# A fused eight-batch attention and FFN kernel: mask row added by VectorE, context loaded transposed, GpSimd's long operations whole, a new order of steps

## The chip, the cores and the metric

The kernel runs on one core of one Trainium2 chip. Its engines are TensorE (PE, with its weight loads as PEld), VectorE (DVE), ScalarE (ACT), GpSimd (POOL) and SyncE (SP), which here only issues DMAs. ACT issues some DMAs too. The metric is the time of one execution on the device in microseconds (us).

## The reference

The reference takes x and a context (both 8 batches x 256 rows x 256 columns, fp32) and a mask row per batch (8 x 256), and applies eight layers to each batch on its own:

```
L0: x += attention(norm(x), ctx), 16 heads    x += top-2-of-8 experts(norm(x)), experts 256x256
L1: x += attention(norm(x), ctx) under a fixed 256x256 mask     x += 3 coupling steps, each a small net
L2: x += linear attention(norm(x), ctx)       x += lin(norm(x)) + gated low-rank experts
L3: x += softmax(q k^T / sqrt(d) + (mask - 1) * 10000) v        x += down(silu(gate) * up), 768 hidden
```

Every attention takes its keys and values from the context. The mask row is the same for all 256 query rows of its batch.

## The kernel before

A batch is 256 rows, held as 2 tiles of 128 partitions (T = 2) with 256 columns; a transposed matrix is 2 column blocks (KT = 2) of 128 partitions with 256 columns. A projection of a batch is four fp32 matmuls on PE, which the trace shows as two records each.

**Threads and order.** On each engine the work is cut into steps by Python generators ("threads"), and `weave` takes one step of a thread after another as a written list says (`TURNS`, lines 89 to 134, one string per engine, one letter per step). The threads: p = `prep` (norm of x, keys, queries and values of the first attention of each batch, the linear attention's context part `third`, keys and values of the second attention), s = `score` (maxima of the head scores, the experts, queries of the second attention), v = `value` (scores again, exponentials, values, output of each attention), a = `net` (the coupling steps and the linear attention), b = `rest` (L2's FFN and all of L3) for batches 0 to 6, c = the same for batch 7 in two halves, w and z = filler matmuls of zeros on PE (line 1986), which keep it running. An engine runs its list strictly in order, so a step whose wait isn't met holds all behind it.

**First attention's context (what the change touches).** `next_cin` (SP, line 499) loads the context of batch b into `cin`. PE's `prepare` (line 1546) starts with `transpose_all` (line 1505) of it, four 128x128 transposes into PSUM; ACT's `prepare` (line 797) copies the result to `ctxT[b % 4]` with a 128x512 copy (`evac`, line 738; the copy is line 740). Buffer b % 4 is free when `rest` of batch b - 4 has done its last read (semaphore `r3_ps`, line 1881). From `ctxT` come all keys and values; `cin` itself is read only by `third` (line 1524).

**Keys and queries** are split into three bf16 parts. ACT makes the first part and an fp32 copy from PSUM; GpSimd makes the others (`split_k`, line 614, `split_q`, line 627): three operations, each once for every column block of 256 columns, so six instructions. SP then writes the parts to a scratch in HBM (line 460) and reads them back as rows of `KA` (line 475) and `QA` (line 493), and the heads of `score` (line 1611) wait for that. For batch 0 the rows are copied directly (`first_keys` by ACT's queue, lines 791 to 795; `first_queries` by SP, line 512, in which SP first waits for the keys to land).

**Norms.** GpSimd's `norm` (line 602) waits for the statistics, makes the reciprocal deviation by two small operations and then, in the same step, waits until DVE has used it (`xh_s`), before it can go on.

**The mask.** In `rest`, DVE turns the mask row, loaded to all 128 partitions, into an additive row and adds a term of the bias (lines 1409 and 1413). PE adds it to the scores by a third matmul, whose weights are the matrix `first` with ones in its first row:

```
for kk in range(KT):
    pe.matmul(ps, L.xhBT[:, kk, t * P:(t + 1) * P], L.k3[:, kk, :], start=(kk == 0), stop=False)
last = pe.matmul(ps, W("first"), L.mrow[:, :], start=False, stop=True)
```

DVE then takes the row maxima by one reduction (line 1446). The attention under the fixed mask has the form that the change takes over: `tensor_tensor_reduce` (line 1169) adds a mask tile to the PSUM scores in place and gives the maximum.

**Large loads.** The packed weights come in seven loads (0 to 3 by SP, 4, 5 and 6 by ACT, line 736); `wi`, the integer weights of L3's FFN, by ACT at line 840, and `dequantize` (line 955) turns it to fp32 in 18 steps.

Of the kernel before, what the change touches and what calls it, by code (L numbers as in the profile page):

```python
# [14 lines left out]
P = 128  # L15
# [28 lines left out]
def cantor_mask():  # L44
# [27 lines left out]
    ("gw3", P, 1), ("aq", P, KT * P), ("first", P, P), ("bao", P, D), ("lin", P, KT * D), ("blin", P, D),  # L72
# [5 lines left out]
for _e in PACK:  # L78
    if _e == "cut":
        CUTS.append(_at)  # L80
    else:
# [17 lines left out]
        "vvbvpsbsabppbaavabavbvvavbvvvbvvvabvpvvbvvabavavvpvvapvavabapvavpvvvvavavvvpsvvvvbvbvvvbvpvvvbvsbbsp"
        "aapvapbavbvavvbavvbvvvvbvvabpavavbvvapvvvvpavavabapavvpavvavvsvvbpvvvbvvbvvpvvvvvvvbvsbbsapapbvapbav"  # L100
        "bvavvbvvavvbvvaabvpvbvvvavvavvavpvvapbavavapvvvpvvavvvavvsvpbvvbvvvbpvvvvbvbsbsapappavbavbavvvvvabvv"
        "vvbvvvvvbvapvbavvbvppvaavpavavapsabavvvvvvaavvvvpbvvvvvbvvvbvvspvsbavbvbvapvvppvbvavbvvavabpvpvvvvav"
        "bvvvvbavavabbvavvavvsvaaabavvvvvaavvvvvbvvsbvvsvvbvcbabbaavavbavvbvavbvvabvavbavbavvvvvavbvavaaavvbv"
        "aavbaabaaaaaabaaaaaaaaabaaaaaaaaaaaaabbaaaabbcccbcbcbcbccbcccccccccccccccccc",
    "vector":
        "ppppppvppppvppppssssssssssssssssssvssvvpvpvpvspspsssssssssssppsssssssssspsssssbssssssssvsvsssssssbpv"
        "svpsssspvsssssssspssvssvsvpvssvasasssssspsssssasasasssssspsspssssvsssssssssasvasapvsppvssssvssaaaaas"
        "apsaabssbvsbpvbbsbbssbbvsvssbbvbaabsssssbbssbssaaassbpssbsssbsssbspsbssssvbsaasvsabssssvvspssvssaaaa"
        "abssapssspapbabsbssbvbbsbbbsbsbbvsbsvpvsssbvpaasbsssbsssbssssbasaabssssbppssbsssbspbsvssasasssbasvss"
        "vsvssssvaaaaabassssbaspabbspspbbbbbbbvsbbssbvsssvsvsbspvapabbssbsssssssbssbaasasbsssbssssspbspbvssss"  # L110
        "vaasabsssvsvsspvssssabaaaasassspsababbpsbsbvbbspbbvbsbsbssbsvsvssbpvapabbsssbsssssssssbsaaassssbsssp"
        "ssbpsssvsbsssbssssvbsvpsvsaaassvbssssaaasaabapsssaabbbpsvbsbsbbbbbpssssvbvbvbvsaspassssbspsssbsbsbss"
        "ssspbsssaaabsvssbsvsssbssssvsvsssbvssbssassaasbssaasaaasbsassababbsssvvsbbbbbbbvvpbbbvaabcssssbsbsbs"
        "sssaaabssbssscbsbsssbaasavbbaaaaavavvbababvabaaabbbbbbbaaaabbbaaaabaaaaaaaaaabbaabacacccbcccccbccccc"
        "bccccbcbcccccbccccccccbcccccccccccccc",
    "tensor":
        "pwwwpppwwwppwwwwwwwppwwwwwwwwwwwwwwwwwwwwwwwwwwwwwwpwwwwwpwpwwwwwwwwppwwwwwwwwwwwwsswpsspssvpsvswwvs"
        "wvvsswwsvswwvpsvvpvpvssvvvvpvpvvvvwwwvwwwvwwwvvwwwwvpvwwvpvvpwwwwwwwpwspsssssssssssssssssppbspsspbps"
        "sbsspssbvssvbssvvpvsbvsbvsspvvbsvpsvpvvvvsspvsvvssvvpvssvsvsvswvpvssvwsvvsswwvwsvpvvpvsvsvsvvsvssvss"
        "vvvvsvspvvsvvsvsvsvvsvsvsvsvvpwwppwaasasspasspsassavsvspsssvvpvpvssavssvvavavssvvspsvsvpvspvvsasvvss"  # L120
        "spavspsavssvvasvpaavspvsavvavavpsvvsvssvsavpsvavvsavsvvvvsvbsvvbvvssvssvssvvsvbsvbpvbvsvpsbsbbaspsas"
        "sbabbvssapavssbapsbbvvssavbbvasvbsvbvpvssavbsbvvsbvbvvapsvsbvsbapsavbsbvbbsvbsvbsvavsavavbsvsbavavap"
        "svsbvppsbvsvpvpvabvavvpvsavssvvvvsbvssbvsssspvvssbvssvbvbssvvpbvsvsbvbvpsvsbsbpasbsasaspspsvassbavps"
        "bbvvasvbsbvpsabbvassvvavsbvbsvvvbsvvbspsababapvspvsbvvbsvbsbsbvbsvsvabsasvavbspvsavavabvpvbpssbvavpa"
        "vpvasvpssvsbvvsbvspvvvbvsvbvbsvvsvssvssvsssvvsbsvbvbvpvsvsbpsbbapssaasppsbsasvbssvbapsbbvasvvsbbvspa"
        "vsbvvbvssavabsbssavvbpvbvpavbvpvvsbsbsvabvsbvbsasvvavsbvavssbvvsavspasvbabvvpvpbsvspvapvvavpvsavvvsb"
        "svbsvsvssvvsvpvsbsbbsvssvsvsbsvssvpbvbsvvbpssbbaspasapsspsasvbsavssbsabvvspvpsvsbavbsvvsavsbvbsvsvvs"
        "vbsvbvvsavspsbvsabspvpsbbvssavvbvbvssabbsvpbvvsabavavpabpsvvabpabspvssvbsvsavvsvasbpvasvvsvbsvbvsvvs"
        "vvssvssvsbvvbbsvpvsvsvvbsspbssbaspsvavsabvpsbbvssvppsavsbsvpsvbpvbavsspvpbbavvvavpvsbvsvsbvvsavsbvsa"
        "vbssvsavsbvsasvbsvvbsbvsasvbbbbbbvavsvbaavssvsabasassbssvbssvvssvbasassvavvvssvvpbvvbvsvsvsvvbvbvbvc"  # L130
        "cvvbcbbacassbassbbavssavscbsavbvbvsasvbbvsavasbbsvavbbasvsbsabvvvvbvabvvavvabvbbabvbabazbbvvbvabvavb"
        "avvzzzzzzzzzbzzzabaaaaazzzzzaaabaaabbaaaaaaaaabaabaabaaaaaaaaaaazzzzzzzzzzzbzzzbbaaaazzzaazzbzzzbbcc"
        "ccbbzzzzzzbbczzzzzzbbzccbbcbbzczzzzcccbcbcccbbbcbccccccccccccccccccccccccccccccc",
# [43 lines left out]
def program(nc, x_in, ctx_in, mask_in, pack, nomask, ipack, scratch, out):  # L177
    ctx = ExitStack()
    with ctx:
# [171 lines left out]
        ctx_ps, ctx_t = sem("ctx_ps", 1), sem("ctx_t", 1)  # L351
# [99 lines left out]
        def _(sp):  # L451
# [118 lines left out]
            def rest():  # L570
                sp.dma_start(mrow[:, :], mask_in[0:1, :].to_broadcast([P, S])).then_inc(m_in_s, 16)
                yield
                for b in range(B - 1):
                    if b + 1 < B - 1:
                        sp.wait_ge(sc_ps, nth(sc_ps, b, 1))
# [7 lines left out]
            sp.dma_start(cin[:, :, :], rows(ctx_in, 0)).then_inc(c_in_s, 16)  # L583
            load(0)
            load(1)
            load(2)
# [7 lines left out]
        def _(pool):  # L594
# [7 lines left out]
            def norm(t, b, n):  # L602
                pool.wait_ge(stats[t], nth(stats[t], b, n))
                link(t, pool.tensor_tensor(veps[t][:, :], mv[t][:, :, 1], epsm[:, :], ALU.add))  # L604
                pool.tensor_tensor(rstd[t][:, :], veps[t][:, :], powm[:, :], ALU.pow).then_inc(rstd_s[t], 1)
                pool.wait_ge(xh_s[t], nth(xh_s[t], b, n))

            def norm_part(t, b, n, h, lo, hi):
# [3 lines left out]
                pool.wait_ge(xh_s[t], of(xh_s[t], b, n, h))  # L612

            def split_k(b, m):
                pool.wait_ge(k_f[m], nth(k_f[m], b, 1))
                for k in range(KT):
                    pool.tensor_tensor(kparts[:, k, 1, :], kf[:, k, :], kparts[:, k, 0, :], ALU.subtract)  # L617
                for k in range(KT):
                    last = pool.tensor_tensor(kf[:, k, :], kf[:, k, :], kparts[:, k, 0, :], ALU.subtract)
                link("p", last)  # L620
                yield
                for k in range(KT):
                    last = pool.tensor_tensor(kparts[:, k, 2, :], kf[:, k, :], kparts[:, k, 1, :], ALU.subtract)
                last.then_inc(k_split[m], 1)
                yield

            def split_q(b, m, t):
                f, parts = qf[m], qparts[m]
                pool.wait_ge(q_f[m], nth(q_f[m], b, 1))
                for k in range(KT):  # L630
                    pool.tensor_tensor(parts[:, k, 1, :], f[:, k, :], parts[:, k, 0, :], ALU.subtract)
                for k in range(KT):
                    last = pool.tensor_tensor(f[:, k, :], f[:, k, :], parts[:, k, 0, :], ALU.subtract)
                link(t, last)
                yield
                for k in range(KT):
                    last = pool.tensor_tensor(parts[:, k, 2, :], f[:, k, :], parts[:, k, 1, :], ALU.subtract)
                last.then_inc(q_split[m], 1)
# [7 lines left out]
            def prepare(b):  # L646
                norm("p", b, 1)
                yield
# [17 lines left out]
            def score():  # L666
                for b in range(B):
                    norm("s", b, 1)
                    yield
                    pool.wait_ge(xh_s["s"], nth(xh_s["s"], b, 1))  # L670
                    for i in range(T):
                        last = pool.tensor_tensor(x[:, i, :], x[:, i, :], xh[:, i, :], ALU.add)
                    last.then_inc(xe_s, 1)
                    yield
                    norm("s", b, 2)
                    yield
# [57 lines left out]
        def _(act):  # L734
# [1362 lines left out]
```

## Time and profile before

| | us |
|---|---|
| three runs | 995.49, 996.83, 1000.37 (median 996.83) |
| the profiled execution | 996.77 |
| its span, first to last instruction | 995.0 |
| PE busy | 957.1 (96%) |
| DVE, ACT, POOL busy | 631.2, 537.3, 235.2 |
| mean granted TensorE clock | 0.997 of full |

All rows below are of this one execution. Times are microseconds from the start of the span unless marked ns. "PE busy" counts fillers as well. A row of the order of time gives start, length, engine, line, operation, output and inputs, shape and how many instructions were merged; square brackets hold the idle time before it and who ended it.

### The profile page before, as it was taken

How to read it: one execution, taken by the hardware profiler on the slowest of the kernel's cores; microseconds unless marked ns; L12 is line 12 of the kernel's file. 1: busy time of each engine (PE TensorE's matmuls, PEld its weight loads, DVE VectorE, ACT ScalarE, POOL GpSimd, SP SyncE). 2: the span in 40 equal slices, each digit the busy share in tenths (PEclk: the TensorE clock that was granted, in tenths of full speed). 3: DMA queues.
4: the chain of work that ended last, by engine and by line, in shares of the span. 5: the costliest groups of instructions: out<-in, count | busy, mean ns of one | idle time of the engine just before them, and what ended most of it. 6: DMA issues, size and time to landing. Idle time of an engine off the chain costs nothing.

```text
span 995.0 us, 17737 instructions
## 1 busy us (share of the span) xinstructions
PE 957.1 (96%) x6202; PEld 711.6 (72%) x6202; DVE 631.2 (63%) x2222; ACT 537.3 (54%) x1103; POOL 235.2 (24%) x418
## 2 busy tenths in 40 slices
PE   8899889989999999999999999999999999999998
PEld 7665565656587867777587766777687867878777
DVE  4634673577677775767576776875676566736554
ACT  1341646496458643766357743776378444864421
POOL 3104402311340241413231043313131113001200
PEclk9999989999999999999999999999999999999999
DMA  7308823120523121402134023402122004000000
GB/s 249 45 14 235 217 49 70 42 55 2 106 49 64 44 53 33 101 11 49 27 68 77 12 48 71 101 17 67 25 43 59 28 1 91 1 13 1 1 1 22
DMA packets 39927, 56.25 MB, mean 57 GB/s; under 512 B 3968, under 2 KB 35712, under 8 KB 36224
## 3 DMA queue, kind: packets, MB, share of 16 engines
q1 hardware_dynamic: 38448, 46.50, 22.8%
q10 hardware_dynamic: 1392, 8.63, 2.4%
q8 instruction: 50, 0.82, 0.4%
q14 instruction: 37, 0.30, 0.1%
HBM read 39.64 MB, written 13.89 MB: 54 GB/s over the span
## 4 chain that ended last, share of the span: by engine, by line
PE 73%; ACT 9%; DVE 6%; DMA 4%; issue 4%; POOL 2%; SPq 1%; ACTq 0%; DVEq 0%; POOLq 0%
PE bank L1639 10%; PE bank L1966 7%; PE bank L1696 6%; PE bank L1499 6%; PE bank L1718 5%; PE bank L1490 5%; PE bank L1977 4%; PE bank L1611 4%; PE bank L1753 4%; PE bank L1747 3%; PE bank L1699 2%; ACT PT L871 2%; PE bank L1508 2%; ACT QA L858 2%; PE bank L1779 2%
## 5 line engine op out<-in xcount | busy, mean ns | idle before, releaser
L871 ACT ACTIVATE PT<-bank 128x512 f32<-128x512 f32 x256 | 153.2, 598 | 140.2 <-PE bank L1699 78.3
L1639 PE MATMUL bank<-w,xhT 128*128 128x512 f32 x256 | 125.2, 598 | 0.0
L1696 PE MATMUL bank<-QA,KA 104*128 104x256 bf16 x512 | 112.8, 273 | 9.2 <-ACT PT L871 6.7
L1169 DVE CUSTOM_DVE_ANT_0 bank<-bank,maskb 128x256 f32<-128x256 f32 x256 | 101.9, 450 | 23.0 <-PE bank L1611 22.2
L1162 DVE TENSOR_REDUCE mx<-bank 128x2 f32<-128x512 f32 x128 | 84.1, 682 | 32.9 <-PE bank L1611 32.2
L1611 PE MATMUL bank<-KA,QA 96*128 96x256 bf16 x512 | 92.9, 275 | 7.6 <-issue 3.0
L1696 PEld LDWEIGHTS bank<-QA,KA 104*128 104x128 bf16 x512 | 46.7, 99 | 57.0 <-issue 45.7
L1966 PE MATMUL bank<-xhBT,wi 128*128 128x256 f32 x336 | 85.2, 384 | 0.7 <-DVE hT L1473 0.3
L1215 DVE SCALAR_TENSOR_TENSOR x<-bank,one,x 128x256 f32<-128x256 f32 x128 | 61.6, 481 | 34.6 <-PE bank L1639 30.0
L858 ACT COPY QA<-bank 8x256 bf16<-8x256 bf16 (+1 forms) x128 | 67.9, 576 | 16.3 <-PE bank L1677 15.0
L1611 PEld LDWEIGHTS bank<-KA,QA 96*128 96x128 bf16 x512 | 47.3, 100 | 31.3 <-issue 6.7
L1966 PEld LDWEIGHTS bank<-xhBT,wi 128*128 128x128 f32 x336 | 58.8, 189 | 10.1 <-DVE hT L1473 3.0
L1699 PE MATMUL bank<-maskb,identb 128*128 128x256 bf16 x256 | 63.5, 273 | 0.0
L1718 PE MATMUL bank<-PT,vaug 128*32 128x256 f32 x1024 | 62.1, 382 | 0.6 <-ACT PT L871 0.6
L1639 PEld LDWEIGHTS bank<-w,xhT 128*128 128x128 f32 x256 | 42.6, 190 | 24.5 <-issue 19.6
L1753 PE MATMUL bank<-xhAT,w 128*128 128x256 f32 (+1 forms) x216 | 49.6, 361 | 1.3 <-ACT xhAT L903 1.0
L1986 PE MATMUL bank<-blank 128*128 128x256 bf16 x348 | 47.0, 282 | 1.1 <-POOL blank L722 1.1
L1718 PEld LDWEIGHTS bank<-PT,vaug 128*32 128x32 f32 x1024 | 29.8, 109 | 24.9 <-issue 7.4
L610 POOL TENSOR_TENSOR veps_a<-mv_a,epsm 128x2 f32<-128x2 f32 (+1 forms) x18 | 3.5, 195 | 171.8 <-DVE mv_a L1052 169.7
L604 POOL TENSOR_TENSOR veps_s<-mv_s,epsm 128x2 f32<-128x2 f32 x16 | 3.2, 197 | 169.6 <-DVE mv_s L1052 168.8
L1264 DVE RECIPROCAL rc<-bank 128x8 f32<-128x8 f32 x64 | 13.0, 204 | 47.5 <-PE bank L1731 47.0
L617 POOL TENSOR_TENSOR kparts<-kf,kparts 128x256 bf16<-128x256 f32 x32 | 20.9, 674 | 90.1 <-ACT kf L756 72.1
(316 smaller groups left out, 2079.8 us busy)
## 6 DMA issues: line engine op xcount, KB each, us to landing
QA<-scratch SPq DMA_DIRECT2D x90, 128.0 KB, 4.4
scratch<-kparts SPq DMA_DIRECT2D x30, 192.0 KB, 2.3
KA<-scratch SPq DMA_DIRECT2D x15, 384.0 KB, 4.6
scratch<-qparts SPq DMA_DIRECT2D x30, 192.0 KB, 2.3
KA<-scratch SPq DMA_DIRECT2D x15, 256.0 KB, 5.5
w<-pack ACTq DMA_DIRECT2D x1, 2409.0 KB, 8.6
wi<-ipack ACTq DMA_DIRECT2D x1, 2304.0 KB, 9.8
xin<-x_in SPq DMA_DIRECT2D x8, 256.0 KB, 5.5
```

Of the source, the lines that this page charges most:

```text
L858: act.copy(QA[m][KR:KM, g * GH + lo:g * GH + hi, :], ot_b16[KR:KM, 512:512 + S].unsqueeze(1).to_broadcast([MR, hi - lo, S])).then_inc(negm ...
L871: act.activation(PT[:, n % RING, :, :].rearrange("p t s -> p (t s)"), st_bank[:, :], ACT.Exp).then_inc(exp_s, 1)
L1162: dve.tensor_reduce(mx[:, i % 4, n % GH, :], s_bank[n % 2][:, :].rearrange("p (t s) -> p t s", t=T), AX.X, ALU.max).then_inc(max_s, 1)
L1169: last = dve.tensor_tensor_reduce(s, s, maskb[:, t, :], op0=ALU.add, op1=ALU.max, scale=1.0, scalar=-HUGE, accum_out=mx[:, i % 4, n % GH, ...
L1215: ins = dve.scalar_tensor_tensor(x[:, t, :], bank[n % 2][:, e * D:(e + 1) * D], one[:, t, k:k + 1], x[:, t, :], ALU.mult, ALU.add)
L1611: last = pe.matmul(s_bank[n % 2][:, t * S:(t + 1) * S], QA[m][0:KR, u, t * P:(t + 1) * P], KA[m][0:KR, u, :], start=True, stop=True)
L1639: last = pe.matmul(bank[n % 2][:, :], xhT[:, kk, t * P:(t + 1) * P], W("exp0", KT)[:, kk, i * 512:(i + 1) * 512], start=(kk == 0), stop=(k ...
L1696: last = pe.matmul(st_bank[:, t * S:(t + 1) * S], KA[m][0:KM, v, t * P:(t + 1) * P], QA[m][0:KM, v, :], start=True, stop=(m == 0))
L1699: last = pe.matmul(st_bank[:, t * S:(t + 1) * S], identb[:, :], maskb[:, t, :], start=False, stop=True)
L1718: last = pe.matmul(pv_bank[32 * h:32 * h + 32, g % 2 * S:(g % 2 + 1) * S], vflat[m][:, t, (g * GH + h) * VW:(g * GH + h) * VW + 32], PT[:, ...
L1753: last = pe.matmul(ps[:, k * S + lo * P:k * S + hi * P], W(name, KT)[:, kk, k * P:(k + 1) * P], src[:, kk, lo * P:hi * P], start=(kk == 0) ...
L1966: last = pe.matmul(ps[:, i * S + lo * P:i * S + hi * P], ww[:, kk, k * P:(k + 1) * P], L.xhBT[:, kk, lo * P:hi * P], start=(kk == 0), stop ...
```

## The change

1. The context also arrives transposed, as an input of its own (`ctxT_in`). SP loads it straight into `ctxT` (eight loads of 256 KB more), and PE's transposes and ACT's copies go. The waits for a free buffer move from ACT to SP. `third` now waits for `cin` itself. At the start `cin` is loaded behind weight load 1, and the transposed context stands in its old place.
2. The mask matmul and the weights `first` go; DVE adds the row with `tensor_tensor_reduce`, one instruction for each half of a batch.
3. GpSimd's split operations and the addition x + xh take both blocks in one instruction of 512 columns.
4. GpSimd's wait for the use of a norm is a step of its own.
5. All five order lists are new.

```diff
 def next_cin(b):
     if b < B:
-        sp.wait_ge(ctx_ps, nth(ctx_ps, b - 1, 1))
+        if b >= CTX:
+            sp.wait_ge(r3_ps, nth(r3_ps, b - CTX, 1))
+        elif b == CTX - 1:
+            sp.wait_ge(qk_ps, 2)
+        if b >= 2:
+            sp.wait_ge(ctx_t[b % 2], nth(ctx_t[b % 2], b // 2 - 1, 16))
+        turned_ctx(b)
         sp.wait_ge(third_pe, nth(third_pe, b - 1, 2))
         sp.dma_start(cin[:, :, :], rows(ctx_in, b)).then_inc(c_in_s, 16)
...
+def turned_ctx(b):
+    sp.dma_start(ctxT[b % CTX][:, :, :].rearrange("p k s -> p (k s)"), ctxT_in[b]).then_inc(ctx_t[b % 2], 16)
...
-    for k in range(KT):
-        pool.tensor_tensor(kparts[:, k, 1, :], kf[:, k, :], kparts[:, k, 0, :], ALU.subtract)
+    pool.tensor_tensor(kparts[:, :, 1, :], kf[:, :, :], kparts[:, :, 0, :], ALU.subtract)
...
-    evac(ctxT[b % CTX], pb if b else lb, ctx_ps, nth(ctx_ps, b, 1), ctx_t)
-    yield
...
-    transpose_all(kb, cin).then_inc(ctx_ps, 1)
-    yield
-    pe.wait_ge(ctx_t, nth(ctx_t, b, 1))
+    pe.wait_ge(ctx_t[b % 2], nth(ctx_t[b % 2], b // 2, 16))
...
-    link(L.t, dve.tensor_reduce(
-        L.m2[:, lo:hi], L.bank[h][:, :].rearrange("p (t s) -> p t s", t=T)[:, lo:hi, :], AX.X, ALU.max))
+    for t in range(lo, hi):
+        ps = L.bank[h][:, t * S:(t + 1) * S]
+        last = dve.tensor_tensor_reduce(ps, ps, L.mrow[:, :], op0=ALU.add, op1=ALU.max, scale=1.0,
+                                        scalar=-HUGE, accum_out=L.m2[:, t:t + 1])
+    link(L.t, last)
...
-    last = pe.matmul(ps, W("first"), L.mrow[:, :], start=False, stop=True)
```

What the new lists say, read letter by letter. PE: 1666 steps for 1680; the order of those that remain is close to the old one (a step shifts by 5 places in the mean, by 103 at most; the first projection of keys of batches 4 to 7 comes some 50 places earlier). Filler steps (two matmuls each): 62 instead of 69 ahead of the first head, 31 in both from there to the experts of batch 0, none in either from there to the first head of attention (0,1), 13 instead of 8 from there on, and 54 instead of 58 at the end. Ahead of the first two heads of attention (1,0) stood the transposes of context 2; now nothing does. ACT: the load of `wi` stood ahead of the exponentials of attention (1,0); now it stands behind the fourteenth of its sixteen, and the first dequantizing step behind the end of that attention. GpSimd: the third key operation of batch 1 stood behind the addition x + xh of the experts of batch 0 and now stands ahead of it; the split of the second attention's keys of batch 0 now starts ahead of the wait for the use of the norm before it. In the new PE list the last read of `ctxT` by `rest` of batch b - 4 stands 82, 64 and 98 places ahead of the first projection of keys of batch b = 5, 6 and 7.

## Rows read from the trace of the kernel before

**Rows 1.** The page: busy time, share of the span, instructions of each engine.

```profile
PE 957.1 (96%) x6202; PEld 711.6 (72%) x6202; DVE 631.2 (63%) x2222; ACT 537.3 (54%) x1103; POOL 235.2 (24%) x418
```

**Rows 2.** Stretches: length, busy time and instructions by engine, clock, DMA share, GB/s.

```profile
75.40:126.30 50.90, 44.07 (x241) 29.11 (x241) 26.05 (x65) 21.13 (x47) 22.23 (x36) 0.99 0.88 222
126.30:250.00 123.70, 114.28 (x757) 76.33 (x758) 79.55 (x307) 75.08 (x151) 26.76 (x46) 0.98 0.21 44
250.00:888.00 638.00, 632.14 (x4067) 473.00 (x4066) 429.51 (x1525) 379.55 (x746) 156.45 (x269) 1.00 0.24 48
```

**Rows 3.** The chain of waits, in order of time: start, length (us), what.

```profile
14.72 3.93 DMA KA<-kparts
```

**Rows 4.** PE in order of time, around the first long stalls.

```profile
103.21 0.66 PE L1508 MATMUL bank<-w,cin 128*128 128x128 f32 x4 [2.22 <-DMA cin<-ctx_in]
103.70 0.60 PE L1611 MATMUL bank<-KA,QA 96*128 96x256 bf16 x4
...
126.31 1.01 PE L1611 MATMUL bank<-KA,QA 96*128 96x256 bf16 x4 [3.03 <-issue]
```

**Rows 5.** The chain of waits between 95 and 116 us.

```profile
95.89 1.31 POOL kparts L617 x2
...
100.27 4.58 DMA scratch<-kparts
...
105.70 10.10 DMA scratch<-qparts
```

**Rows 6.** ACT's queue in order of time: the load of wi.

```profile
105.22 0.41 ACTq L840 DMA_DIRECT2D wi<-ipack  x1
```

**Rows 7.** A stretch of 25 us; after the engines come clock, DMA share, GB/s.

```profile
125.00:150.00 25.00, 22.61 (x155) 15.51 (x156) 19.33 (x94) 10.55 (x25) 0.89 (x2) 0.86 0.23 46
```

**Rows 8.** PE in order of time, last batch: mask matmul and what follows it.

```profile
963.99 0.59 PE L1928 MATMUL bank<-xin,w 128*128 128x256 f32 x2
964.42 1.03 PE L1927 MATMUL bank<-kf,xh0T 128*128 128x256 f32 x4
```

**Rows 9.** DVE groups by line and shape: busy us and mean ns, idle before.

```profile
L1169 DVE CUSTOM_DVE_ANT_0 bank<-bank,maskb 128x256 f32<-128x256 f32 x256 | 101.9, 450 | 23.0 <-PE bank L1611 22.2
...
L1446 DVE TENSOR_REDUCE m<-bank 128x2 f32<-128x512 f32 x7 | 4.8, 684 | 2.2 <-PE bank L1928 2.2
```

**Rows 10.** PE's instructions of line 1881 alone, by stretches of 10 us.

```profile
350.00:360.00 10.00, 1.03 (x4) 0.68 (x4) 1.00 0.04 8
```

**Rows 11.** All engines in order of time, the first 36 us.

```profile
6.51 1.11 PE L1508 MATMUL bank<-w,cin 128*128 128x128 f32 x4 [1.81 <-DMA w<-pack]
...
7.74 0.39 ACTq L736 DMA_DIRECT2D w<-pack  x1
...
8.70 2.20 PE L1490 MATMUL bank<-ctxT,w 128*128 128x256 f32 x8
```

**Rows 12.** DMA issues of the whole span: count, KB each, median us to landing.

```profile
QA<-scratch SPq DMA_DIRECT2D x90, 128.0 KB, 4.4
...
w<-pack ACTq DMA_DIRECT2D x1, 2048.0 KB, 10.2
```

**Rows 13.** SP's queue in order of time: the reads of attention (1,0).

```profile
94.68 2.63 SPq L493 DMA_DIRECT2D QA<-scratch  x6
```

**Rows 14.** GpSimd in order of time around the third key operation of batch 1.

```profile
75.58 1.41 POOL L672 TENSOR_TENSOR x<-x,xh 128x256 f32<-128x256 f32 x2 [0.91 <-DVE xh L1065]
76.94 1.30 POOL L623 TENSOR_TENSOR kparts<-kf,kparts 128x256 bf16<-128x256 f32 x2
```

**Rows 15.** GpSimd groups by line and shape.

```profile
L617 POOL TENSOR_TENSOR kparts<-kf,kparts 128x256 bf16<-128x256 f32 x32 | 20.9, 674 | 90.1 <-ACT kf L756 72.1 <-DVE xh L1065 17.9
...
L604 POOL TENSOR_TENSOR veps_p<-mv_p,epsm 128x2 f32<-128x2 f32 x8 | 1.6, 196 | 87.3 <-DVE mv_p L1052 87.1
```

**Rows 16.** The filler matmuls (line 1986) alone, by stretches.

```profile
126.30:250.00 123.70, 2.73 (x16) 1.51 (x16) 0.98 0.21 44
```

More of the change, by code:

```diff
@@ L99 @@
[L99 to L103, printed above, removed]
@@ L174, in weave, with program @@
             pass
-def program(nc, x_in, ctx_in, mask_in, pack, nomask, ipack, scratch, out):
+def program(nc, x_in, ctx_in, ctxT_in, mask_in, pack, nomask, ipack, scratch, out):
     ctx = ExitStack()
@@ L349, in program @@
         xh_s = {t: sem(f"xh_{t}", n) for t, n in norms.items()}
-        ctx_ps, ctx_t = sem("ctx_ps", 1), sem("ctx_t", 1)
+        ctx_t = [sem(f"ctx_t{i}", 16) for i in range(2)]
         xh0T_ps, xh0T_s = sem("xh0T_ps", 1), sem("xh0T_s", 1)
@@ L582, in _ @@
             sp.dma_start(xin[0][:, :, :], rows(x_in, 0)).then_inc(x_in_s[0], 16)
-            sp.dma_start(cin[:, :, :], rows(ctx_in, 0)).then_inc(c_in_s, 16)
+            turned_ctx(0)
             load(0)
             load(1)
+            sp.dma_start(cin[:, :, :], rows(ctx_in, 0)).then_inc(c_in_s, 16)
             load(2)
@@ L611, in norm_part @@
                 pool.tensor_tensor(rstd[t][:, lo:hi], veps[t][:, lo:hi], powm[:, lo:hi], ALU.pow).then_inc(rstd_s[t], 1)
-                pool.wait_ge(xh_s[t], of(xh_s[t], b, n, h))
             def split_k(b, m):
                 pool.wait_ge(k_f[m], nth(k_f[m], b, 1))
-                for k in range(KT):
-                    pool.tensor_tensor(kparts[:, k, 1, :], kf[:, k, :], kparts[:, k, 0, :], ALU.subtract)
-                for k in range(KT):
-                    last = pool.tensor_tensor(kf[:, k, :], kf[:, k, :], kparts[:, k, 0, :], ALU.subtract)
-                link("p", last)
+                pool.tensor_tensor(kparts[:, :, 1, :], kf[:, :, :], kparts[:, :, 0, :], ALU.subtract)
+                link("p", pool.tensor_tensor(kf[:, :, :], kf[:, :, :], kparts[:, :, 0, :], ALU.subtract))
                 yield
-                for k in range(KT):
-                    last = pool.tensor_tensor(kparts[:, k, 2, :], kf[:, k, :], kparts[:, k, 1, :], ALU.subtract)
-                last.then_inc(k_split[m], 1)
+                pool.tensor_tensor(kparts[:, :, 2, :], kf[:, :, :], kparts[:, :, 1, :], ALU.subtract).then_inc(k_split[m], 1)
                 yield
@@ L629, in split_q @@
                 pool.wait_ge(q_f[m], nth(q_f[m], b, 1))
[L630 to L634, printed above, removed]
+                pool.tensor_tensor(parts[:, :, 1, :], f[:, :, :], parts[:, :, 0, :], ALU.subtract)
+                link(t, pool.tensor_tensor(f[:, :, :], f[:, :, :], parts[:, :, 0, :], ALU.subtract))
                 yield
-                for k in range(KT):
-                    last = pool.tensor_tensor(parts[:, k, 2, :], f[:, k, :], parts[:, k, 1, :], ALU.subtract)
-                last.then_inc(q_split[m], 1)
+                pool.tensor_tensor(parts[:, :, 2, :], f[:, :, :], parts[:, :, 1, :], ALU.subtract).then_inc(q_split[m], 1)
                 yield
@@ L647, in prepare @@
                 norm("p", b, 1)
+                yield
+                used("p", b, 1)
                 yield
@@ L669, in score @@
                     yield
+                    used("s", b, 1)
+                    yield
                     pool.wait_ge(xh_s["s"], nth(xh_s["s"], b, 1))
-                    for i in range(T):
-                        last = pool.tensor_tensor(x[:, i, :], x[:, i, :], xh[:, i, :], ALU.add)
-                    last.then_inc(xe_s, 1)
+                    pool.tensor_tensor(x[:, :, :], x[:, :, :], xh[:, :, :], ALU.add).then_inc(xe_s, 1)
                     yield
                     norm("s", b, 2)
+                    yield
+                    used("s", b, 2)
                     yield
@@ L708, in rest @@
                         norm_lane(L, b, 1, h, lo, hi)
+                        yield
+                        used_lane(L, b, 1, h)
                         yield
@@ L1926, in rest @@
                             for kk in range(KT):
-                                pe.matmul(ps, L.xhBT[:, kk, t * P:(t + 1) * P], L.k3[:, kk, :], start=(kk == 0), stop=False)
-                            last = pe.matmul(ps, W("first"), L.mrow[:, :], start=False, stop=True)
+                                last = pe.matmul(ps, L.xhBT[:, kk, t * P:(t + 1) * P], L.k3[:, kk, :],
+                                                 start=(kk == 0), stop=(kk == KT - 1))
                             if t + 1 < hi:
@@ L2063, in packed @@
         "right": padded(a["L2_ffn_right"].reshape(E * R, D), P, D),
-        "first": padded(np.ones((1, P), np.float32), P, P),
         "wq3t": tiles(a["L3_xattn_Wq"].T), "bq3": column(a["L3_xattn_bq"]),
@@ L2083 @@
         "ctx_in": np.ascontiguousarray(a["ctx_1024"]),
+        "ctxT_in": np.stack([tiles(c.T) for c in a["ctx_1024"]]),
         "mask_in": np.ascontiguousarray(a["mask_BxS2_ff1"]),
```

102 lines of the change are left out of this document (59 added, 43 removed).

## The prediction

> **What bounds the kernel now.** I read first the busy shares and the stretches, then the chain of waits and PE's order of time in the start, then the queues' issues around the one long stall. PE is busy 96% of the span [rows 1]. By stretches [rows 2] it idles 6.83 us in 75.4 to 126.3, 9.42 us in 126.3 to 250 and 5.86 us in the 638 us to 888. Before the first and behind the last of these, filler matmuls (line 1986) count as busy, so there the bound is the chain of waits; from 126.3 to 888 it is PE itself, and every other engine has room (DVE 429.5 of 638 us).
>
> The start has three waits that matter. The first attention's heads wait for rows of KA and QA sent by DMA; the head of that chain is the ACT-issued copy of the first keys, which landed at 18.65 (14.72 + 3.93) [rows 3]. At 103.21 PE, after 2.22 us idle, transposes context 2, and only behind that, at 103.70, does it start the heads of attention (1,0) [rows 4]. And at 126.31, after 3.03 us idle, it starts the heads of (0,1) [rows 4]: their queries' write to scratch took 10.10 us from 105.70 [rows 5], in a stretch where ACT had issued the 2304 KB load of wi at 105.22 [rows 6]. Around that idle the granted clock fell from 2.4 to 1.2 GHz: it was 0.86 in 125 to 150 [rows 7], so 7.0 us were spent at the lower level.
>
> **The change part by part.** The sum is made on the profiled execution: 996.77 us, of which 995.0 is span and 1.77 lies around it; the median of the runs is 996.83.
>
> *Mask matmuls.* 16 leave PE (two a batch). Start to start one costs 964.42 - 963.99 = 0.43 us [rows 8]; the busy column says 0.59 because it overlaps the next. Six batches have theirs between 126.3 and 888: 12 x 0.43 = 5.2 us, on the path as PE is the bound there. The other four (batches 6 and 7) lie after 888 in dense PE work: 1.7 us. Bounds: 0.43 and 0.59 each, so 6.9 to 9.4. In their place DVE reads each half with the add-and-max instruction, 450 ns, and a short read of the accumulator: twice 450 for one reduction of 684 [rows 9], +0.2 to +0.5 us a batch. DVE has 208 us free in 250 to 888 [rows 2], and the lane that waits (rest) has a batch's time of slack, so I count 0; in the last batch, where nothing covers it, 0.2 us, beside 0.86 us of mask there, within the 1.7.
>
> *Context transposes and their copies.* Four transposes a batch: 0.49 us (103.21 to 103.70) [rows 4]. Five batches (3 to 7) have theirs after 126.3: 2.4 us (0.49 and 0.66 each, 2.4 to 3.3). The ACT copy that goes with each leaves an engine with room: 0. In exchange SP issues eight more loads of 256 KB, one a batch. Batches 4 to 7 now wait on SP for the rest lane of four batches before. For batch 5 that lane's last reader of the context ran in 350 to 360 [rows 10]. Counting turns in the new lists, SP is held at this wait for some 30 of them, but what stands next on it (the second queries of batch 3) is not ready before PE has made 66 more turns, and the first keys of batch 5 come 82 turns after the release (a turn is 995/1680 = 0.59 us, so 48 us). For batches 6 and 7 it is 64 and 98 turns. So nothing waits: 0.
>
> *Start, to 37.3.* The projection of the first keys began at 8.70, after transposes at 6.51 and their copy [rows 11]: 2.2 us earlier now. But ACT also issues load 4 (2048 KB) 1.2 us earlier, and it is the same queue that carries the first keys: issued at 7.74 [rows 11], landing 10.2 us after [rows 12], so near 18.1, and the keys landed 18.65. There are also 256 KB more ahead of it. I take 0.3 of the 2.2, bounds -0.6 and 2.2.
> The trace has the keys land 0.5 us behind the load [rows 3, 12]. The Trainium skill, DMA: Bandwidth & Descriptors (Queues, rings and completion order), says that each DMA engine takes the descriptors of one queue in order. By that rule the earlier copy can't pass the load and this term is near 0, the sum 0.3 smaller; were it not so, it is 2.2.
>
> *Heads (1,0).* PE's new order has no transposes there, and the heads no longer stand behind cin: -2.7 us if their QA rows have landed. SP issued these from 94.68 to 97.3 [rows 13]; GpSimd does the third key operation of batch 1 ahead of the 1.41 us addition to x instead of behind it [rows 14], and SP's chain starts from that at 78.3, so all moves 1.4 us up. Such a row takes 4.4 us to land [rows 12], so 101.7 becomes 100.3, and PE is free at 100.99. I take 2.5; bounds 0.4 and 2.7. The price here is 256 KB more in a busy stretch, behind the QA rows.
>
> *Heads (0,1).* In ACT's new list the load of wi stands behind the fourteenth exponential of attention (1,0), past the write that it slowed; PE's heads (0,1) begin before that. Without it the queries' write, 10.10 us, should come near the 4.58 us that the keys' write took just before [rows 5]: 5.5 us, more than the 3.03 us stall plus the 2.5 us that PE comes earlier is worth. I take 2.5 of the 3.03 (0 to 3.0). With the idle goes the low clock: of the 7.0 us at most 1.3 lie in the idle, so some 5.8 us of work ran at half rate, 2.9 us lost; I take 2.5 (0 to 2.9). What is late next: the dequantizing on ACT, which waits for wi and has the next attention's exponentials behind it; some seven heads at 1.2 us lie between, 8 to 9 us against 9.8 us of landing, so up to 1.5 us of stall, inside the bounds.
>
> *GpSimd, whole operations.* An operation on 256 columns takes 674 ns and one on 2 columns 196 [rows 15], so 1.88 ns a column, and 512 take 1.16 us against 1.31 for a pair in the chain [rows 5]. Six pairs are in the chain to heads (0,1), -0.9 us, already inside the terms above; in the PE-bound part 0. Bounds 0 and 1.
> The Trainium skill, GPSIMD Engine Reference (3.1 Elementwise), gives about 2.6 cycles an element at 1.2 GHz for two-input operations; by that slope 512 columns are an estimated 1.30 us and the whole form gains nothing (that chain is 0.9 us later). The trace's slope is lower.
> Waits for xh as turns of their own: they free GpSimd for other work early; the one that stood ahead of the split of the second keys of batch 0 held it till 95.89 [rows 5], under 1 us, which is counted above.
>
> *New order.* Aside from what was said, PE's list is nearly the old one (mean shift of a step 5 turns). Filler turns: 62 for 69 before the first head, 13 for 8 after heads (0,1), 54 for 58 at the end. Five more in the middle cost at most 5 x 0.34 = 1.7 us [rows 16]; as they fill idle time in part I count +0.7.
>
> **Sum:** 0.3 + 2.5 + 2.5 + 2.5 + 5.2 + 2.4 + 1.7 - 0.7 = 16.4 us. 995.0 - 16.4 + 1.8 = 980.4 us; against the median of the runs the same.
>
> **Rivals.**
> A, the stall before heads (0,1) stays, because other traffic (the added context load, cin, xin, the scratch writes) fills the DMAs there anyway: they were busy 88% of 75.4 to 126.3 [rows 2]. PE then only waits longer and the clock falls as before. Lost: 5.0 and, as a start later absorbed, the 2.5 of heads (1,0): 16.4 - 7.5 = 8.9, 988 us. For it: the keys' own write was slow before wi was issued. Against: 10.10 is twice 4.58, and wi is the one large load there.
> B, all bounds at the good end: the mask at 0.59 and the transposes at 0.66, the start's 2.2 whole and the stall whole: 9.4 + 3.3 + 2.2 + 2.7 + 5.9 = 23.5 less 0.7 is 22.8, 974 us. Against: start-to-start times.
> C, the gain is eaten by order. PE's 15.3 us idle between 126.3 and 888 [rows 2] is small because the old list fits the old durations; with steps shifted by up to 100 turns it doubles: 996.8 - 16.4 + 15.3 = 995.7, no change.
> D, slower: SP held at the new wait for the rest lane before the context load of batches 4 to 7. If that lane's r3 step comes so late that the load lands behind the turn of the batch's first key projection, PE stops in order, as at 126.31. Price per stop: 3.03 idle and 2.9 of low clock, 5.9 us, and four of them 23.6: 996.8 - 16.4 + 23.6 = 1004. It decides once r3 comes within some 6 us (issue and landing) of that projection; the count above gives 38 us or more, so little speaks for it.
>
> **How the numbers follow.** The forecast 0.60, A 0.15, B 0.10, C 0.09, D 0.06. The forecast's own range is 976 to 986; with A and half of B, and leaving out C and D, 973 to 991. About 0.5% (5 us) is what a measurement tells from no change: faster holds the forecast, A and B, 0.85; same is C, 0.09; slower is D, 0.06.
>
> **What would show it.** No transposes of cin and no mask matmul on PE; GpSimd operations of 512 columns near 1.16 us; first heads within 1 us of 37.3; heads (1,0) near 101 and heads (0,1) near 120.5 to 121.5 with no fall of the clock; between that and the start of the last batch's tail 7 to 8 us less. Wrong if heads (0,1) still come behind 3 us of idle and a clock of 0.5, if PE idle after them is over 20 us, or if the first heads come 2 us early.

## The result, and the profile after

Four runs of the changed kernel: 984.87 to 987.86 us, median 987.23, beside 998.06 for the kernel before on the same chip: ratio 0.9892 with a 95% interval of 0.9868 to 0.9917, some 10.8 us less. The prediction was 980.4 us (16.4 less), range 973 to 991. The profiled execution took 987.86 us with a span of 986.1.

The busy line of the page after, and the three stretches that answer to [rows 1, 2] (columns as there):

```profile
PE 949.3 (96%) x6126; PEld 702.7 (71%) x6126; DVE 634.1 (64%) x2245; ACT 536.3 (54%) x1097; POOL 221.5 (22%) x317
```

```profile
75.40:126.30 50.90, 48.21 (x257) 32.01 (x257) 30.61 (x86) 21.75 (x48) 17.59 (x20) 0.97 0.68 159
126.30:250.00 123.70, 115.25 (x785) 77.00 (x788) 76.98 (x291) 75.79 (x152) 27.48 (x35) 0.99 0.32 72
250.00:880.00 630.00, 620.83 (x3982) 462.89 (x3973) 431.52 (x1538) 378.78 (x740) 143.59 (x196) 1.00 0.24 49
```

PE's idle time in 75.4 to 126.3 fell from 6.8 to 2.7 us. In the long middle it rose: 9.2 us in 630, where [rows 2] have 5.9 in 638. PE in order of time, at the two places of [rows 4]:

```profile
101.55 0.61 PE L1629 MATMUL bank<-KA,QA 96*128 96x256 bf16 x4
...
120.92 0.60 PE L1629 MATMUL bank<-KA,QA 96*128 96x256 bf16 x4
```

Heads (1,0) start 2.15 us earlier and heads (0,1) 5.4 us earlier, with no idle before them. By about 132 us, where the third attention of batch 2 begins (before: 138.96, now: 131.79), 7.2 us are won. That is four fifths of the 8.9 us by which this span is shorter, in the first seventh of it. At the first matmul of `net`'s last product (line 1829 before, 1847 now) the gain is 8.8 us for batch 6 (898.08 before, 889.33 now) and 7.7 for batch 7.

### The profile page after: what moved, and what is told of

Same layout as the page of the kernel before. It is cut to its first block, busy times and chain, and to the rows that moved or that the text cites. A ratio compares the mean times of both kernels' runs of the same rounds, so it can differ in the third digit from the quotient of the medians.

```text
span 986.1 us, 17493 instructions
## 1 busy us (share of the span) xinstructions
PE 949.3 (96%) x6126; PEld 702.7 (71%) x6126; DVE 634.1 (64%) x2245; ACT 536.3 (54%) x1097; POOL 221.5 (22%) x317
## 4 chain that ended last, share of the span: by engine, by line
PE 77%; ACT 9%; DVE 8%; issue 4%; POOL 1%; DMA 1%; ACTq 0%; SPq 0%; DVEq 0%; POOLq 0%
PE bank L1657 11%; PE bank L1984 6%; PE bank L1517 6%; PE bank L1736 6%; PE bank L1714 6%; PE bank L1508 6%; PE bank L1629 4%; PE bank L1995 4%; PE bank L1771 4%; PE bank L1765 3%; PE bank L1717 3%; ACT PT L886 2%; ACT QA L873 2%; PE bank L1797 2%; PE bank L1526 2%
## 5 line engine op out<-in xcount | busy, mean ns | idle before, releaser
L2004 PE MATMUL bank<-blank 128*128 128x256 bf16 x336 | 44.7, 279 | 1.1 <-POOL blank L743 1.1
L1995 PE MATMUL bank<-wi,hT 128*128 128x256 f32 x168 | 42.2, 382 | 0.1
```

The costliest lines, as they stand in the source:

```text
L1995: last = pe.matmul(ps[:, t * D:(t + 1) * D], hid[:, kk, t * P:(t + 1) * P], wd[:, kk, :], start=(kk == 0), stop=(kk == HT - 1))
```

## The experiments

"Before" and "after" below are the two kernels; ratios are to before, on the same chip. Batches are numbered from 0. A gain "at batch n" is the time by which that batch's first matmul of line 1829 (1847 after) comes earlier than in the profile of before. "Lost clock" is the sum of (1 - granted clock) over windows of 1 us within the span: a fall to 1.2 GHz for 3.4 us loses 1.7.

**Each edit by itself, every list in its old order.** Mask row only (SP's wait before it overwrites the mask row goes with it, from PE's scores to DVE's maxima):

```diff
-    last = pe.matmul(ps, W("first"), L.mrow[:, :], start=False, stop=True)
+    (DVE)  dve.tensor_tensor_reduce(ps, ps, L.mrow[:, :], op0=ALU.add, op1=ALU.max, ...)
```

> The kernel before with one edit: the mask row is added by VectorE in one tensor_tensor_reduce per query tile, and the mask matmul is gone; the order of every engine is the old one. Theory 1 (the terms of the prediction: every mask matmul stood on a path that TensorE sets): 12 x 0.43 us in batches 0 to 6 and 1.7 us in the tail, 6.9 us less, a ratio near 0.993. Rival (TensorE waits for ScalarE's exponentials and VectorE's maxima anyway, so most of the freed time turns idle): under 3 us less, 0.997 to 1.000, with more idle time ahead of the second scores in the waits.

Measured: 0.9981 (0.9964 to 0.9997), 1.9 us less. Transposed context only:

```diff
-    transpose_all(kb, cin)        # and ACT's copy of it
+    sp.dma_start(ctxT[b % CTX]..., ctxT_in[b])
```

> The kernel before with one edit: the transposed context is loaded, TensorE's transposes and ScalarE's eviction of them are gone, the rest of each engine's order is the old one, and the big MLP weight load stays ahead of attention (1,0). Theory 1: 0.3 at the start, 2.4 us for five batches' transposes, up to 2.5 at the heads of (1,0): about 5 us less at the end, 0.995, and the stall before the heads of (0,1) still there, about 3 us long with the clock falling after it. Rival (the start gives its 2 us and the stall takes them, the transposes filled idle time): 0 to 2 us less, 0.998 to 1.000.

Measured: 0.9997 (0.9976 to 1.0018). GpSimd's operations whole only:

```diff
-    for k in range(KT): pool.tensor_tensor(kparts[:, k, 1, :], kf[:, k, :], kparts[:, k, 0, :], ...)
+    pool.tensor_tensor(kparts[:, :, 1, :], kf[:, :, :], kparts[:, :, 0, :], ...)
```

> The kernel before with one edit: GpSimd's splits and its sum whole with 512 columns; each wait for the normalized rows stays in its old place. Theory 1: 0.15 us less per pair (1.16 against 1.31), nothing of it on the path: 1.000, within 0.1%. Rival (the splits of the keys stand on the chain to the heads, and the shared port makes VectorE slower beside a long operation): a change of over 2 us either way.

Measured: 0.9999 (0.9981 to 1.0016). And the three together, still in the old order:

> The kernel before with all three edits (mask row, transposed context, whole operations) in the old order of every engine, the load of the MLP weights in its old place too. Theory 1 (the parts add up): the sum of the three kernels above, by the prediction's terms 12 us less, 0.988, so that the new order with the later load brings little over it, against the 5 us that the stall and its clock were put at. Rival (the parts share one limit, ScalarE's exponentials or the stall): less than the sum, 4 to 7 us less, 0.993 to 0.996, and the new order brings the rest.

Measured: 0.9982 (0.9961 to 1.0004), 1.8 us less. So for the mask and for the context the rival holds, for GpSimd the first theory, and the three together bring less than even their rival's 4 to 7 us: of the 12 us that the terms give the parts, the old lists pay out two. Why is seen where the kernel with the mask edit and the kernel before, whose PE steps stand in the same order, are laid side by side. PE in order of time, near 390 us, before:

```profile
387.41 1.02 PE L1927 MATMUL bank<-hT,xhBT 128*128 128x256 f32 x4
388.27 0.59 PE L1928 MATMUL bank<-mrow,w 128*128 128x256 f32 x2
...
390.44 1.03 PE L1499 MATMUL bank<-w,attT 128*128 128x256 f32 x4
391.31 0.29 PE L1537 MATMUL bank<-w,xh0T 128*128 128x16 f32 x2
391.72 0.66 PE L1508 MATMUL bank<-w,xh 128*128 128x128 f32 x4
```

and the same steps with the mask row on DVE (PE's lines are 3 higher), PE's rows with one each of GpSimd and DVE between them:

```profile
387.19 1.02 PE L1930 MATMUL bank<-hT,xhBT 128*128 128x256 f32 x4
...
389.38 1.13 PE L1502 MATMUL bank<-w,attT 128*128 128x256 f32 x4
389.99 0.69 POOL L605 TENSOR_TENSOR rstd_s<-veps_s,powm 128x2 f32<-128x2 f32 x1
390.35 0.29 PE L1540 MATMUL bank<-w,xh0T 128*128 128x16 f32 x2
390.71 0.73 DVE L1065 TENSOR_SCALAR xh<-x,mv_s,rstd_s 128x256 f32<-128x256 f32 x2 [1.15 <-POOL rstd_s L605]
391.50 0.66 PE L1511 MATMUL bank<-w,xh 128*128 128x128 f32 x4 [0.86 <-DVE xh L1065]
```

The lead is 0.22 us ahead of the mask step and 1.06 behind it: the 0.84 us are really won. Three steps later PE stands 0.86 us for DVE's normalized rows `xh`, and the lead is 0.22 again. Those rows are the end of a chain (the last expert's matmuls, DVE's sum and statistics, GpSimd's rstd, DVE's scaling) that started from PE ahead of the mask step and is as much earlier as PE was there; the mask matmuls lay under that chain. In the kernel before, the rows were ready at 391.67 and PE came for them at 391.72: the list fitted to 0.05 us. The same is seen in the other batches: each gains 0.4 to 0.9 us at its mask step and meets a wait soon after, for `xh` at 613 us (0.73), for `xhA` at 729 and 840 us (0.47 and 0.63); only near 500 us some 0.3 us are kept. In that kernel PE waits 1.6 us for `xh` and 1.1 for `xhA` between 250 and 880 us, for which before it did not wait, and the milestone's gain goes from 0.2 at batch 1 to 0.4 at batch 5, with eight mask matmuls (3.4 us) gone between. The rival named other waits, for ScalarE's exponentials and VectorE's maxima; those hardly changed (2.3 us for the exponentials before, 2.4 now).

**The load of wi.** The kernel before, the load some ten steps later in ACT's list:

```diff
-  "...bbsspbsvvbvvvpvpvpvvvvpvvvvvb..."
+  "...bbsspbvvbvvvpvpvpvvvvspvvvvvb..."     # scalar; s = load of wi
```

> The kernel before with one edit: ScalarE issues the load of the MLP weights ten steps later in its list, after the seventh to eighth exponential of attention (1,0), near 120 us instead of 105.2; nothing else differs. Theory 1 (the load's 2.5 MB stood in the queues ahead of the keys and queries of (0,1)): the 3.0 us of idle before the heads of (0,1) and the half clock after it go, 5 us less at the end (0.995). Rival (those us were cover: another wait, DVE's or ScalarE's, takes the next place, or the first dequantize now waits for the load and holds ScalarE at 130 us): 0 to 1.5 us less.

Measured: 1.0006 (0.9988 to 1.0023). It went as the rival says; ACT, then PE, in order of time:

```profile
128.88 0.42 ACT L955 ACTIVATE wi<-wi 128x256 f32<-128x256 int32 x1 [3.11 <-DMA wi<-ipack]
```

```profile
122.90 0.60 PE L1611 MATMUL bank<-KA,QA 96*128 96x256 bf16 x4
...
129.93 0.59 PE L1696 MATMUL bank<-QA,KA 104*128 104x256 bf16 x2 [2.97 <-ACT PT L871]
```

Heads (0,1) come 3.4 us earlier without a stall; then the first dequantize, at its old place, waits for the load, and an exponential stands behind it. Moved along with the load:

> The kernel before with two moves in ScalarE's list: the load of the MLP weights near 120 us, and the first six dequantize steps behind the exponentials that they stood ahead of (from 130 us to 136 and later), so that none waits for the load; nothing else differs. In the run with the load alone moved the 3.0 us stall was gone, and ScalarE then waited 3.1 us for the load at its first dequantize and TensorE 3.0 us for the exponential behind it. Theory 1 as amended (the stall is worth its time only if the dequantize steps go with the load): 3 to 5 us less, 0.995 to 0.997. Rival (the next wait is only a little later, by the once-per-batch waits for VectorE): 1.000, milestones of batch 1 equal.

Measured: 0.9969 (0.9943 to 0.9994), 3.1 us less; the gain is 2.1 to 2.3 us from batch 1 to 6. So the change's two moves in ACT's list belong together. The same beside the three edits, first with the load alone:

> The kernel before with the three edits (mask row, transposed context, whole operations) and the load of the MLP weights at the later place, all else in the old order. Against the kernel with the three edits alone (2 us less than before). Theory 1 (the load is what matters in the new order): 5 us more, 7 in all, 0.993, and the rest to the change's 10.8 is the lists' doing. Theory 3 (in the old lists TensorE waits once per batch for VectorE's normalized rows, which the removed matmuls had covered, so that time won early is kept only up to the next such wait): the stall goes and the milestones of the batches after it stand 5 to 8 us earlier, flat to 880 us. Rival to both: the stall's time is given back before 250 us, under 3 us in all.

Measured: 1.0021 (1.0002 to 1.0040), 3.19 us of idle ahead of the same exponential. With both moves:

> The kernel before with the three edits (mask row, transposed context, whole operations) and both moves in ScalarE's list, all other lists old. Theory 1 as amended (parts add up): 2 us of the three edits and 3 to 5 of the moves, 5 to 7 us less, 0.993 to 0.995; what is left to the change's 10.8 us, 4 to 6 us, is the worth of the rest of the new order. Theory 3 (the old lists give time won back at once-per-batch waits): the win of the moves is kept, since it is ahead of them all, but the mask matmuls' and transposes' 7.6 us are not, so never below 0.993.

Measured: 0.9971 (0.9953 to 0.9989), 2.9 us less. That misses the first theory, which had 5 to 7: edits worth 1.8 and moves worth 3.1 give 2.9 together. What is missing to 10.8 us, some 8 us, is then the rest of the new order (with it GpSimd's wait for a norm as its own step and the other filler turns, which no run separates). Most of it is won early: in the profiles the new order is ahead of this kernel by 3.7 us where the third attention of batch 2 begins, by 6.3 at batch 1 and by some 6.5 at the end. From the first heads to batch 1 it takes 6.6 us less; PE idles 3.4 us less there (16.3 for 19.8) and 3.4 us less of clock is lost (3.4 for 6.8), which is all of it in these two profiles. The opposite test, the load back early in the new order:

> The kernel after the change with one edit: the load of the MLP weights back ahead of attention (1,0) in ScalarE's list (near 105 us instead of 126.7), all else in the new order. Theory 1: the stall is back, 2 to 3 us of idle before the heads of (0,1) and the clock at half for 3.4 us after it, 3 to 5 us more than after the change (0.992 to 0.994 of before). Rival (the new order issues the keys and queries of (0,1) before the load's bytes matter, or the stall is made up by 250 us): within 1 us of after the change, 0.989.

Measured: 0.9957 (0.9937 to 0.9978). This edit moved more than the load: its turn went in ahead of five others of the same thread, and each of these came one turn earlier. ACT now took the copy of E0's second transposes before the keys of (0,1). ACT in order of time:

```profile
97.97 0.58 ACT L761 COPY xhT<-bank 128x512 f32<-128x512 f32 x1 [19.26 <-PE bank L1526]
98.45 0.48 ACT L775 ACTIVATE kparts<-bank,w 128x256 bf16<-128x256 f32 x1
```

After the change these keys are evicted from 91.82 on. By 120.6 us 6.3 us were lost to that and to the clock; the stall before heads (0,1), the thing asked for, was 1.23 us. So 0.9957 is no price of the load, and the run shows only that the stall then comes back in part.

**GpSimd's halves.** The traces show what the prediction had not looked at. All engines after the change, near 740 us:

```profile
738.85 1.16 POOL L634 TENSOR_TENSOR kparts<-kf,kparts 128x512 bf16<-128x512 f32 x1 [10.15 <-ACT kf L777]
738.88 1.27 DVE L1318 SCALAR_TENSOR_TENSOR o<-xhA,cn 128x128 f32<-128x128 f32 x1
...
739.96 1.20 POOL L635 TENSOR_TENSOR kf<-kf,kparts 128x512 f32<-128x512 f32 x1
740.07 1.24 DVE L1318 SCALAR_TENSOR_TENSOR o<-xhA,cc 128x128 f32<-128x128 f32 x1
...
741.24 1.30 DVE L1318 SCALAR_TENSOR_TENSOR o<-xhA,cn 128x128 f32<-128x128 f32 x1
741.24 1.15 POOL L637 TENSOR_TENSOR kparts<-kf,kparts 128x512 bf16<-128x512 f32 x1
...
742.90 0.42 DVE L1491 TENSOR_TENSOR hT<-sg,bank 128x256 f32<-128x256 f32 x1
...
743.38 1.46 PE L1984 MATMUL bank<-xhBT,wi 128*128 128x256 f32 x4 [2.01 <-DVE hT L1491]
```

DVE's sum takes 0.35 us (its median); three in a row take 1.27, 1.24 and 1.30, each as long as the GpSimd operation that runs beside it. `hT`, which PE waits for, stands behind them in DVE's list, PE idles 2.01 us, and its clock falls. The Trainium skill, SBUF — State Buffer (SBUF: two separate sides), says that these two engines share one pair of ports, and that when a DVE instruction has two SBUF inputs and a GpSimd one reads SBUF, the one that starts first holds the pair for its whole length while the other blocks. This sum has two SBUF inputs and the GpSimd operation reads SBUF; these rows agree. The longest such excess on one DVE operation was 0.6 us before and 1.0 after. The kernel after the change with halves again:

```diff
-    pool.tensor_tensor(kparts[:, :, 1, :], kf[:, :, :], kparts[:, :, 0, :], ALU.subtract)
+    for k in range(KT):
+        pool.tensor_tensor(kparts[:, k, 1, :], kf[:, k, :], kparts[:, k, 0, :], ALU.subtract)
```

> The kernel after the change with one edit: GpSimd's splits and its sum again in halves of 256 columns, every list in the new order. Theory 2 (found in the traces, not in the prediction: while a GpSimd operation runs, VectorE's operations with operands in SBUF wait for its end, up to 1.0 us beside a whole one and 0.6 beside a half): VectorE's lengthened operations go from 15.7 us to about 12, none of its 128x128 sums takes over 0.9 us, TensorE's wait of 2.0 us near 741 shrinks below 1.2 with no clock fall after it: 2 to 4 us less (0.996 to 0.998). Rival (theory 1, no effect off the path; a pair of halves is 0.15 us longer and its consumers later): 0.999 to 1.002, and the wait near 741 stays.

Measured: 983.63 us, 0.9861 (0.9839 to 0.9884), 3 us less than after the change; the intervals of the two overlap, and they were not timed side by side. Near 740 us:

```profile
741.48 0.79 DVE L1330 SCALAR_TENSOR_TENSOR o<-xhA,cn 128x128 f32<-128x128 f32 x1
742.20 0.75 DVE L1330 SCALAR_TENSOR_TENSOR o<-xhA,cc 128x128 f32<-128x128 f32 x1
742.87 0.75 DVE L1330 SCALAR_TENSOR_TENSOR o<-xhA,cn 128x128 f32<-128x128 f32 x1
...
744.47 0.70 PE L1996 MATMUL bank<-xhBT,wi 128*128 128x256 f32 x2 [0.49 <-DVE hT L1503]
```

The wait is 0.49 us and no fall of the clock follows it. All that DVE's operations took over their own medians (where over 0.1 us) sank only from 16.2 to 15.3 us: it is the one collision on the path that counted. In the old order the whole operations lengthened DVE's more (13.1 us before, 19.8 with them) and cost nothing (0.9999): none of these stood where PE waited.

**Fillers where the clock fell.** The kernel after the change had four falls inside its span, at 95, 218, 744 and 904 us; two stretches show two of them (columns as in [rows 2]):

```profile
95.00:100.00 5.00, 5.00 (x18) 4.12 (x19) 0.00 (x0) 1.08 (x6) 2.06 (x2) 0.66 0.99 187
...
743.00:747.00 4.00, 3.62 (x12) 2.64 (x13) 2.88 (x6) 0.60 (x1) 0.63 (x2) 0.63 0.78 186
```

```diff
-  ... kq.1, E0.xhT2 ...              # tensor, the steps in words
+  ... kq.1, 5 x filler, E0.xhT2 ...  # and 1 and 2 fillers near 900 and 904 us
```

> The kernel after the change with TensorE's filler matmuls (of no result) added where its clock fell: 10 in the idle 1.3 us ahead of the transposes of E0 at 95 us, 2 and 4 ahead of two steps of the last batch's network near 900 and 904 us; nothing else differs. Theory C (each fall costs half of the 3.4 us that it lasts, 1.7 us, and comes from the idle just before it): the falls at 95 and 904 us gone, 3 us less (0.997). Rival (a later wait takes the time at 95 us, since the heads of (1,0) or their maxima are bound elsewhere, and the fillers cost their own 0.1 us each where TensorE was not idle): 0.999 to 1.001.

Measured: 985.87 us, 0.9893 (0.9869 to 0.9916): 1.4 us less than after the change in the median, half of what theory C gave, but the same in the ratio, so the times don't decide. Its trace has the falls at 95 and 904 us gone, the other two still there, and a span 2.1 us shorter. Halves and fillers together:

> The kernel after the change with GpSimd's operations in halves again and TensorE's filler matmuls (of no result) at five places: 10 ahead of the transposes of E0 at 95 us, 6 ahead of the third attention's first projection at 23 us (taken from the 38 ahead of the first heads), 2 and 4 in the last batch's network. Theories 2 and C add up: 3.6 us less from the halves and 1.4 from the fillers than after the change, 982 us, 0.984 to 0.985, a granted clock of 0.997 or more. Rival (both took away the same clock falls): no better than the halves alone, 0.986.

Measured: 982.18 us, 0.9835 (0.9805 to 0.9865), the fastest of all, 5 us below the change. Beside halves alone (0.9839 to 0.9884) its interval overlaps, so the fillers' own share is not shown by the times. The two stretches above, now of PE alone (busy, clock, DMA share, GB/s):

```profile
95.00:100.00 5.00, 5.00 (x27) 1.00 0.99 163
743.00:747.00 4.00, 4.00 (x47) 1.00 0.76 188
```

The step that waits for `hT` stands at 741.5 us there, behind 0.48 us of idle.

What the profiled executions add up to:

| kernel | ratio | span | lost clock | gain at batch 1, 5 |
|---|---|---|---|---|
| before | 1 | 995.0 | 3.4 | 0, 0 |
| mask only, old order | 0.9981 | 995.6 | 8.5 | 0.2, 0.4 |
| context only, old order | 0.9997 | 995.5 | 10.2 | 1.1, 1.2 |
| three edits, old order | 0.9982 | 993.1 | 8.5 | 3.0, 2.7 |
| three edits and both moves | 0.9971 | 992.6 | 8.5 | 1.7, 1.5 |
| after | 0.9892 | 986.1 | 6.8 | 8.0, 9.2 |
| after, halves | 0.9861 | 984.1 | 5.1 | 5.9, 9.8 |
| after, halves and fillers | 0.9835 | 981.1 | 1.7 | 8.8, 12.7 |

Two readings. Between batch 1 and 5 (some 355 to 811 us) no clock was lost in the rows of the old order nor in the last two: the same removed matmuls gain -0.3 us there in the old lists (0.1 each for the two edits apart, with GpSimd in halves) and +3.9 in the new ones. PE's idle time there was 3.5 us before, 6.3 with the three edits in the old order and 4.0 with halves and fillers in the new one.

The other is on the lost clock, and there one profile misleads: that of before is one of its good executions. Worked out from the granted clock of every run, before lost 5.8 to 6.8 us in the mean (23 to 35 runs beside the groups of kernels), the mask alone 6.1, the three edits 8.1, these with both moves 8.8, after 6.0, after with halves 3.6 and with fillers too 1.7. So the new order lost less clock than the same edits in the old one, and with halves, and with halves and fillers, 2.4 and 4.3 us less was lost than after, of leads of 3 and 5 us. A start can also be late in one profile: that of halves lost 3.4 us to a fall at 26 us, hence its 5.9 at batch 1.

## Why the prediction was partly right

*Heads (0,1), 2.5 us and 2.5 of clock: right in size, with a condition missed.* 120.92 lies in the forecast 120.5 to 121.5, without stall or fall. The late dequantizing that the prediction named was what undid the load's move by itself (3.11 us of ACT's idle against the 1.5 allowed); the new lists avoid it.

*Start, 0.3 us: wrong.* The first heads came at 35.32 instead of 37.26, the case that the text called wrong. In the nine kernels with the context edit they came at 34.7 to 35.8 (39.1 in the one with the fall at 26 us), in the five without at 36.3 to 37.7. The first keys landed later (20.52 for 18.65), but not because of the load ahead of them in their own queue, by which the prediction reasoned: that load landed earlier (17.39 for 17.94), and the keys 3.1 us behind it. SP's last weight load, in another queue, landed at 19.58 for 17.91; that it held the keys is not shown. And the heads did not hang on the keys. The last transfer they wait for is SP's copy of the queries, before and now, with PE's first heads:

```profile
28.07 2.82 SPq L518 DMA_DIRECT2D QA<-QA  x3
37.26 0.60 PE L1611 MATMUL bank<-KA,QA 96*128 96x256 bf16 x4 [2.10 <-DMA QA<-QA]
```

```profile
25.93 3.25 SPq L528 DMA_DIRECT2D QA<-QA  x3
35.32 0.60 PE L1629 MATMUL bank<-KA,QA 96*128 96x256 bf16 x4
```

The queries' chain got the whole 2 us, with the context edit alone too (first heads at 35.26). The step that failed is "the head of that chain is the ACT-issued copy of the first keys". *Heads (1,0), 2.5:* only 0.2 beyond the start's 2.0, so the cumulative 2.15 against 2.8. By 132 us the errors had cancelled: 7.2 for 7.8, which is luck in part.

*Mask 5.2 and transposes 2.4: the step that lacked a condition.* "On the path as PE is the bound there" took PE's 99% busy for proof that a matmul less is time less. In the old order the mask kernel shows 0.1 us where 3.4 were taken out. PE was full, but a chain through DVE and GpSimd closed on it in each batch, and the removed work lay under that chain. Only steps put under it in a new order turn the gap into time: with halves, whose profile has no fall there, the new lists gain 5.5 us between the third attention of batch 2 and batch 6, of the 6.9 (7.6 less 0.7) forecast. The prediction counted the new order as fillers, +0.7, and "nearly the old one"; by the runs it carries some 8 of the 10.8 us, most of them ahead of batch 1.

*The middle, 7.6 less 0.7 expected: about 1.6 us seen up to batch 6.* In the profile after, two falls (218 and 744 us, 1.7 each) and the wait of 2.0 us at 743 cost 5.4 of it. The wait and the fall behind it, 3.7 of these, go with the whole GpSimd operations: the term "in the PE-bound part 0". Their duration was forecast well (1.16 us; measured 1.15 to 1.17). The 1.30 us estimated from the slope that the Trainium skill gives, GPSIMD Engine Reference (3.1 Elementwise), was too long. But what a longer operation does to DVE's beside it was not priced. It was worth some 3 us in the runs, net of what the shorter chain gains. Rival C (gain eaten by order, idle doubled) was half there: middle idle 9.2 for 5.9. *Tail, 1.7:* from batch 6 to the end 0.2, with the fall at 904 us (1.7) in it.

Rival A's time (988) is the nearest to the measured 987.2, but not its mechanism: no stall was left. D's wait on SP cost nothing; no wait of PE for the transposed context is among those in the trace. The sum came out 5.6 us too large, and the mechanism was right for the stall, not for the middle.

## What to carry to other kernels

An engine at 99% is not yet the bound: ask which chain through the other engines returns to it in each period, and whether the work that goes away lies under it. Price such an edit only together with the list that fills the gap, and price a moved load together with its first reader. Where GpSimd and DVE both work on SBUF, keep GpSimd's operations short if a DVE result beside them is waited for; elsewhere their length cost nothing here.

## What the runs showed of the hardware

- A DVE sum with two SBUF inputs took up to the whole length of the GpSimd operation beside it: 1.24 to 1.30 us for a 0.35 us sum beside 512 columns (1.15 to 1.20), 0.75 to 0.79 beside halves (0.67).
- After the change PE's granted clock fell to 1.2 GHz after idle of 1.32 us (95 us) and 2.01 us (743 us); ten fillers ahead of the transposes at 95 us kept that one away. The length of the idle alone does not decide: ahead of the first heads, behind a run of fillers, the clock stayed up after 2.10 us in the profile before and fell after 1.98 us in the one with the load back early. A fall that lies whole in a span lost 1.7 us of clock, twice or three times that.
- Executions of one kernel spread by up to 12 us (992.49 to 1004.06 for the 29 of before beside the last four kernels), wider than most edits here. A good part goes with the clock: the ten of these with a mean granted clock of 0.991 had a median of 1000.3 us, the seven with 0.997 one of 997.0. What sets how many falls an execution has was not tested.
